# A recommender tower's cross layers: layer 1's fourth unit of products made in halves through PSUM and split in two parts, and the accumulators' banks used by the chunk's parity

## What is computed

```python
for W, b in params:                       # 4096, 8192, 8192 products; 128 outputs each
    z = jnp.einsum('bhd,bfd->bhfd', x_vec, input)
    B, h, f, d = z.shape
    z = z.reshape(B, h * f, d)
    x_vec = jnp.einsum('oc,bcd->bod', W, z) + b[None, :, None]
    outs.append(x_vec.sum(axis=2))
```

## Time and profile before

| | us |
|---|---|
| three runs | 1167.61, 1166.23, 1167.39; median 1167.39 |
| the profiled execution, its own time | 1163.56 |
| its span | 1161.6 |
| busy in the span: TensorE, DVE, POOL, ACT | 1098.8, 1011.0, 905.4, 688.7 |
| TensorE's granted clock over the span | 0.997 |

### The profile page before, as it was taken

One profiled execution on the slowest core, in us unless ns is written; L12 is line 12 of the kernel. 1 busy time (PEld: TensorE's weight loads), 2 busy tenths in 40 slices (PEclk: granted clock), 3 DMA queues, 4 the chain that ended last, 5 costly groups with the idle time before them and its releaser, 6 DMA issues.

```text
span 1161.6 us, 13994 instructions
## 1 busy us (share of the span) xinstructions
PE 1098.8 (95%) x4276; PEld 744.5 (64%) x4276; DVE 1011.0 (87%) x670; ACT 688.7 (59%) x712; POOL 905.4 (78%) x403
## 2 busy tenths in 40 slices
PE   0479999999999999999999999999999999999998
PEld 0246666666666666667666666666676666666696
DVE  4599899999999999989999999999899999998452
ACT  5365466665656656665566666566656566566443
POOL 6469989888988888888988888888889887567000
PEclk9989999999999999999999999999999999999999
DMA  6642415334262525143352524252442525142891
GB/s 239 185 124 66 114 49 153 93 100 145 67 169 75 152 64 161 47 150 94 81 156 73 164 79 136 72 159 57 126 118 79 155 75 159 57 148 88 292 355 41
DMA packets 101789, 142.87 MB, mean 123 GB/s; under 512 B 11746, under 2 KB 55010, under 8 KB 98947
## 3 DMA queue, kind: packets, MB, share of 16 engines
q1 hardware_dynamic: 93570, 140.42, 39.3%
q0 software_dynamic: 8192, 2.11, 2.3%
HBM read 114.96 MB, written 27.53 MB: 123 GB/s over the span
## 4 chain that ended last, share of the span: by engine, by line
PE 84%; POOL 7%; DVE 3%; issue 3%; ACT 2%; DMA 1%; SPq 0%; ACTq 0%; DVEq 0%
PE acc L1110 49%; PE acc L1104 25%; POOL emb L574 3%; POOL z_lo L583 3%; PE z_ps L1251 3%; PE turn_gram_ps L1179 3%; PE z_ps L1241 1%; DVE z L654 1%; DVE z_float L654 1%; ACT x L901 1%; PE turn_gram_ps L1166 1%; DVE z_ps L660 1%; PE acc L1136 1%; DVE z_lo L666 1%; DMA land<-x_scratch 0%
## 5 line engine op out<-in xcount | busy, mean ns | idle before, releaser
L583 POOL TENSOR_TENSOR z_lo<-z,z_hi 128x2048 fp32r<-128x2048 f32 x143 | 659.8, 4615 | 104.4 <-ACT z_hi L864 102.2
L1104 PE MATMUL acc<-z_float,w_sb 128*128 128x512 f32 x768 | 348.7, 600 | 56.8 <-DVE z_float L654 43.2
L1110 PE MATMUL acc<-z_hi,w_hi 128*128 128x512 f32 x896 | 378.3, 422 | 2.5 <-POOL z_lo L583 1.6
L1110 PE MATMUL acc<-z_hi,w_lo 128*128 128x512 f32 x896 | 353.7, 395 | 0.0
L1110 PE MATMUL acc<-z_lo,w_hi 128*128 128x512 f32 x896 | 353.3, 394 | 0.0
L864 ACT ACTIVATE z_hi<-z 128x2048 fp32r<-128x2048 f32 x144 | 275.2, 1911 | 60.5 <-DVE z L654 60.5
L574 POOL DMA_INDIRECT emb<-in_tables,rows_chunk x256 | 245.3, 958 | 63.8 <-issue 56.4
L1104 PEld LDWEIGHTS acc<-z_float,w_sb 128*128 128x128 f32 x768 | 145.7, 192 | 213.0 <-issue 199.0
L873 ACT ACTIVATE z_hi<-z_ps 128x1024 fp32r<-128x1024 f32 x160 | 164.5, 1028 | 127.1 <-PE acc L1110 72.7
L666 DVE TENSOR_TENSOR z_lo<-z_ps,z_hi 128x1024 fp32r<-128x1024 f32 x160 | 194.5, 1216 | 32.5 <-ACT z_hi L873 32.5
L654 DVE TENSOR_TENSOR z<-operand_even,x_shift 128x2048 f32<-128x2048 f32 x80 | 182.9, 2286 | 38.6 <-PE acc L1110 16.2
(11 more groups left out here) (117 smaller groups left out, 631.9 us busy)
## 6 DMA issues: line engine op xcount, KB each, us to landing
land<-x_scratch SPq DMA_DIRECT2D x128, 256.0 KB
land<-x_scratch SPq DMA_DIRECT2D x128, 128.0 KB
x_shift<-x_scratch SPq DMA_DIRECT2D x16, 1024.0 KB, 5.8
gram_scratch<-gram SPq DMA_DIRECT2D x32, 512.0 KB, 6.5
x_shift<-x_scratch SPq DMA_DIRECT2D x16, 768.0 KB, 8.1
z_float<-gram_scratch SPq DMA_DIRECT2D x7, 1024.0 KB, 9.5
x_scratch<-emb SPq DMA_DIRECT2D x32, 192.0 KB, 2.8
x_shift<-gram_scratch SPq DMA_DIRECT2D x6, 1024.0 KB, 6.4
```

What stands on the lines that cost most here:

```text
L583: pool.tensor_tensor(z_lo[:, slot], z[:, slot], z_hi[:, slot].bitcast(F32), ALU.subtract).then_inc(subtracted, 1)
L1104: mm = pe.matmul(acc[:, :], weights[:, tile0 + q, :], z_float[:, g.float_slot(pos), q, :], start=start and q == 0, stop=stop and q == QUAD ...
L1110: mm = pe.matmul(acc[:, :], w[:, tile, :], zz[:, slot, q, :], start=False, stop=stop and n == 2)
```

## The change

Layer 1's position 3 becomes a second unit made in halves. DVE forms it in two halves into `z_ps`, ACT rounds each half, DVE subtracts, and TensorE takes it by `halves_unit` from the same single slot. The subtractions and other products are put in a new order in `layer1_middle`, which now takes up to four pieces of work to place between. Semaphore counts follow (`products`, `halves`, `halves_units`). `z_float` holds one unit a group. The weights of the fourth unit move from the plain to the split arrays, which take 4096 bytes a partition against 2048 before; the area for descriptors of dynamic DMAs shrinks from 8192 to 4096. The two accumulators become `acc[0]` and `acc[1]`: both layers of a chunk use the bank of its parity. Layer 1 of a chunk then waits for x2 of two chunks before, and layer 2 for x1 of the same chunk. In the start, the wait for all split weights moves ahead of layer 1 of chunk 1.

```diff
...
 SPLIT_UNITS = 3
-L1_SPLIT = 2 * QUAD
+L1_SPLIT = SPLIT_UNITS * QUAD
 L2_SPLIT = L2_GROUPS * SPLIT_UNITS * QUAD
 SPLIT_TILES = L1_SPLIT + L2_SPLIT
-L1_PLAIN, L2_PLAIN = 2 * QUAD, L2_GROUPS * QUAD
+L1_PLAIN, L2_PLAIN = QUAD, L2_GROUPS * QUAD
 FLOAT_SLOTS, UNIT_SLOTS = 2, 3
...
+    def products(self, more=0):
+
+        groups, layer1 = self.before()
+        return self.chunk.count(3 * GROUPS - 1, 3 * groups - layer1 + more)
+
+    def halves(self, more=0):
+
+        groups, layer1 = self.before()
+        return self.chunk.count(2 * GROUPS + 2, 2 * groups + 2 * layer1 + more)
+
+    def halves_units(self, more=0):
+
+        groups, layer1 = self.before()
+        return self.chunk.count(GROUPS + 1, groups + layer1 + more)
+
     def unit_slot(self, pos):
...
-    def float_slot(self, pos):
+    def float_slot(self):
         groups, layer1 = self.before()
-        return (groups + layer1 + pos // 3) % FLOAT_SLOTS
+        return (GROUPS * self.chunk.par + groups) % FLOAT_SLOTS
...
-        acc1 = ps("acc1", [P, COLS])
-        acc2 = ps("acc2", [P, COLS])
+        acc = [ps("acc_even", [P, COLS]), ps("acc_odd", [P, COLS])]
...
-                is_float = pos == 0 or pos == 3 and g.is_layer1
-                freed = g.float_freed(pos) if is_float else g.unit_freed(pos)
+                freed = g.unit_freed(pos) if pos else g.float_freed()
                 if freed is not None:
                     dve.wait_ge(used, freed)
-                out = z_float[:, g.float_slot(pos)] if is_float else z[:, g.unit_slot(pos)]
+                out = z[:, g.unit_slot(pos)] if pos else z_float[:, g.float_slot()]
                 dve.tensor_tensor(out, *times(bank, QUAD, x0_tiles), ALU.mult).then_inc(formed, 1)
-            def form_half(g, half, bank, x0_tiles):
-
-                if not g.is_first or half:
-                    dve.wait_ge(halves_split, g.count(2, half))
+            def form_half(g, half, bank, x0_tiles, pos=2):
+
+                n = 2 * (pos - 2) + half
+                if not g.is_first or n:
+                    dve.wait_ge(halves_split, g.halves(n))
                 dve.tensor_tensor(z_ps[:, :, :], *times(bank, 2, x0_tiles), ALU.mult).then_inc(halves_formed, 1)
-            def split_half(g, half):
-
-                dve.wait_ge(halves_rounded, g.count(2, half + 1))
+            def split_half(g, half, pos=2):
+
+                dve.wait_ge(halves_rounded, g.halves(2 * (pos - 2) + half + 1))
                 tiles = slice(2 * half, 2 * half + 2)
...
                 else:
-                    form_half(g, half, pair % 2, x0_shift[:, c.par, 1 + 2 * half:3 + 2 * half])
+                    form_half(g, half, pair % 2, x0_shift[:, c.par, 1 + 2 * half:3 + 2 * half], pos)
...
-            def layer1_middle(c):
-                layer1(c, 2, half=0)
-                layer1(c, 3)
-                split_half(layer1_group(c), 0)
-                layer1(c, 2, half=1)
+            def layer1_middle(c, *between):
+
+                g = layer1_group(c)
+                for n, (pos, half) in enumerate(((2, 0), (2, 1), (3, 0), (3, 1))):
+                    layer1(c, pos, half=half)
+                    if n < len(between):
+                        between[n]()
+                    split_half(g, half, pos)
...
                 split_half(layer2_group(c, 1), 1)
-                sum2(prev)
                 layer1(nxt, 0)
-                split_square(nxt)
-                layer1_middle(nxt)
-                layer2(c, 2, 1)
-                split_half(layer1_group(nxt), 1)
-                layer2(c, 2, 0)
+                layer1_middle(nxt, lambda: split_square(nxt), lambda: sum2(prev),
+                              lambda: layer2(c, 2, 1), lambda: layer2(c, 2, 0))
                 layer2_middle(c, 2)
...
             layer1(c0, 0)
-            split_square(c0)
-
             dve.wait_ge(rounded, 1)
...
                               ALU.subtract).then_inc(subtracted, 1)
-            layer1_middle(c0)
-            split_half(g0, 1)
+            layer1_middle(c0, lambda: split_square(c0))
             layer1(c1, 1)
             layer1(c1, 0)
-            split_square(c1)
-            layer1_middle(c1)
-            split_half(layer1_group(c1), 1)
-            sum1(c0)
+            layer1_middle(c1, lambda: split_square(c1), lambda: sum1(c0))
             layer2(c0, 0, 1)
...
             def released_by_layer2(g, bank):
-                return (formed, g.count(3, 2)) if bank == 0 else (halves_formed, g.count(2, 2))
+                return (formed, g.products(2)) if bank == 0 else (halves_formed, g.halves(2))
             def released_by_layer1(g, bank):
-                return (halves_formed, g.count(2, 2)) if bank == 0 else (formed, g.count(3, 3))
+                return halves_formed, g.halves(2 + 2 * bank)
...
-                act.wait_ge(formed, g.count(3, pos))
+                act.wait_ge(formed, g.products(pos))
                 act.activation(z_hi[:, g.unit_slot(pos)], z[:, g.unit_slot(pos)], ACT.Copy).then_inc(rounded, 1)
-            def round_half(g, half):
-                act.wait_ge(halves_formed, g.count(2, half + 1))
-                if not g.is_first:
+            def round_half(g, half, pos=2):
+                act.wait_ge(halves_formed, g.halves(2 * (pos - 2) + half + 1))
+                if not (g.is_first and pos == 2):
                     if half == 0:
-                        act.wait_ge(half_used, g.count(1))
+                        act.wait_ge(half_used, g.halves_units(pos - 2))
+                    elif pos == 3:
+                        act.wait_ge(used, g.count(4, 3))
                     else:
-                        act.wait_ge(used, g.count(4, -1))
+                        act.wait_ge(used, g.count(4, 0 if g.layer1_at(1) else -1))
                 act.activation(z_hi[:, HALVES_SLOT, 2 * half:2 * half + 2], z_ps[:, :, :], ACT.Copy).then_inc(halves_rounded, 1)
...
                 to_bank(m, 1, 1, released_by_layer2(b, 1))
-                to_bank(m, 2, 0, (formed, m.count(3, 1)))
+                to_bank(m, 2, 0, (formed, m.products(1)))
                 round_unit(m, 1)
-                to_bank(m, 3, 1, (formed, m.count(3, 2)))
+                to_bank(m, 3, 1, (formed, m.products(2)))
                 round_half(m, 0)
...
                 round_half(m, 1)
+                round_half(m, 0, 3)
                 to_bank(d, 1, 1, released_by_layer1(m, 1))
+                round_half(m, 1, 3)
                 round_unit(d, 1)
...
             act.wait_ge(top_in, 6 * 16)
-            for m, bank in enumerate((acc1[:, :], operand[0][:, :], operand[1][:, :], z_ps[:, 0, :])):
+            for m, bank in enumerate((acc[0][:, :], operand[0][:, :], operand[1][:, :], z_ps[:, 0, :])):
                 act.wait_ge(top1_done, m + 1)
...
             act.wait_ge(top3_done, 1)
-            act.activation(y_sb, acc2[0:1, :], ACT.Copy).then_inc(y_ready, 1)
+            act.activation(y_sb, acc[1][0:1, :], ACT.Copy).then_inc(y_ready, 1)
...
         def _(pe):
-            def float_unit(g, acc, weights, tile0, pos=0, start=False, stop=False):
-
-                pe.wait_ge(formed, g.count(3, 2 if pos == 0 else 3))
+            def float_unit(g, acc, weights, tile0, start=False):
+
+                pe.wait_ge(formed, g.products(2))
                 for q in range(QUAD):
-                    mm = pe.matmul(acc[:, :], weights[:, tile0 + q, :], z_float[:, g.float_slot(pos), q, :],
-                                   start=start and q == 0, stop=stop and q == QUAD - 1)
+                    mm = pe.matmul(acc[:, :], weights[:, tile0 + q, :], z_float[:, g.float_slot(), q, :],
+                                   start=start and q == 0, stop=False)
                 mm.then_inc(used, 1)
...
-            def halves_unit(g, acc, tile0):
+            def halves_unit(g, acc, tile0, pos=2, stop=False):
                 for half, done in enumerate((half_used, used)):
-                    pe.wait_ge(halves_split, g.count(2, half + 1))
+                    pe.wait_ge(halves_split, g.halves(2 * (pos - 2) + half + 1))
                     for q in (2 * half, 2 * half + 1):
-                        mm = split_tile(acc, tile0 + q, HALVES_SLOT, q, False)
+                        mm = split_tile(acc, tile0 + q, HALVES_SLOT, q, stop and q == QUAD - 1)
                     mm.then_inc(done, 1)
...
                 g = layer1_group(c)
-                if not c.is_(0):
-                    pe.wait_ge(x1_ready, c.count(1))
-                float_unit(g, acc1, w0_sb, 0, start=True)
-                split_unit(g, 1, acc1, 0)
+                if not (c.is_(0) or c.is_(1)):
+                    pe.wait_ge(x2_ready, c.count(1, -1))
+                float_unit(g, acc[c.par], w0_sb, 0, start=True)
+                split_unit(g, 1, acc[c.par], 0)
                 pe.wait_ge(square_split, c.count(1, 1))
                 for part in range(2):
-                    pe.matmul(acc1[:, :], w_sq[:, part, :], z_sq[:, :], start=False, stop=False)
```

(31 more changed lines are left out.)

30 lines of the change are left out of this document (15 added, 15 removed).

## The result

| | before | after |
|---|---|---|
| median | 1166.32 (6 runs, 1165.95 to 1167.61) | 1271.65 (6 runs, 1267.37 to 1273.98) |
| the profiled execution, own time and span | 1163.56, 1161.6 | 1273.98, 1272.0 |
| granted clock over the span | 0.997 | 0.965 |

The account below looks back on a forecast made before the run. TensorE was taken to bound the kernel, at 64.3 us a round. Twelve intervals at +4.4 (52.8), the last +3.0, start 7.8 and end 3.2 made +66.8 on 1163.56: 1230.4, so a median of 1234; range 1213 to 1264.

Parts of the forecast that it names:

- what the halves and POOL's cycle cost: Chunk 2's m2 to chunk 15's: twelve intervals at +4.4 us (52.8), the last, by TensorE's chain, at +3.0.
- the start: Before the steady rounds: POOL's first layer 2 unit comes later because its product stands behind chunk 1's m3; +7.8 us.
- behind chunk 15's squares: After chunk 15's m2: 8.52 us to d0 where it was 1.40 + 3.47, less an x2 wait; +3.2 us.
- What it adds to DVE and ACT: Each round: DVE gains 2.6 us, to 62.4, plus some 1.8 of waits; ACT gets two roundings of 1.03 us.
- The new wait: At m3's two halves, behind m2 in the single slot: TensorE waits 1.14 and 3.18 us, making a round 67.3.
- What queues behind the wait: ACT's in-order work delays d1: POOL begins it at 7.2 us and closes the cycle at 68.7 us a round.
- Halved descriptor area: POOL's lookups: the smaller area was taken to cost 0, with up to 24 us left to the range.
- The rival that the halves hide: At m3's two gaps: both halves ready in time, only savings stay, about 1148 us; 5%.
- the one that POOL does not close: In the rounds: POOL's pace holds slack the chip does not need; +50 us, a median of 1217; 17%.
- DVE being late elsewhere is excluded by that margin of 3 us: In the rounds: DVE's 62.4 + 1.8 us of its own fits in 67.3, so it reaches the waiting subtraction in time.
- the list of ACT's work behind m3's roundings: ACT's queue in a round: m3's roundings, operand copy, then `round_unit` of d1 (1.91 us), done at about 7.2 us.
- The clock rival: TensorE's clock falls in the new gaps of m3: 2.7 us lost a round, +88, a median of 1255; 26%.

Follow-up runs that it names:

- fill: The changed kernel with DVE's subtraction for the squares' low part replaced by a memset to zeros: 1246.56 us, ratio 1.0709 to the kernel before.
- earlier copy: The changed kernel with the fill, and ACT's second Gram copy moved right behind the first, ahead of d3's rounding: 1242.79 us, ratio 1.0667.
- fillers: 3 and 11 zero-weight matmuls put ahead of TensorE's waits for m3's halves: on the fill alone 1261.14 us, on fill plus earlier copy 1238.12 us.

## Why the prediction was right in kind and wrong in size

The 43.6 us between +66.8 as summed and +110.4 as profiled are found as follows; the terms of the 13 rounds are differences of their landmarks between runs.

| term | forecast | measured |
|---|---|---|
| 13 rounds, what the halves and POOL's cycle cost (fill, earlier copy, fillers) | 55.8 | 59.3 |
| the clock, once the Gram wait is away (earlier copy without and with fillers) | 0 | 2.9 |
| the Gram copy (fill against earlier copy) | 0 | 7.3 |
| z_sq against POOL (change against fill) | 0 | 18.9 |
| the start | 7.8 | 15.6 |
| behind chunk 15's squares | 3.2 | 6.5 |

No run holds the clock still between these rows, so each difference carries some of it: of the 18.9, 2.3 us lie in the two first rounds, whose subtraction is short, and 2.1 of the 7.3 are the two rounds of 70.5. By the subtraction in its old place the z_sq term is 21.3.

**What holds.** "What it adds to DVE and ACT": 2.6 us a round more on DVE, 62.4, measured 62.2 to 62.4. "The new wait": 0.97 and 2.92 for 1.14 and 3.18 in the rounds without a long subtraction. "What queues behind the wait": POOL begins d1 at 758.58, 7.20 after zero, as forecast to the hundredth, and closes the cycle at 68.86 us for 68.7 as soon as nothing else is in the way. "Halved descriptor area": zero. The rival that the halves hide has fallen, and so has the one that POOL does not close.

**The step that failed** is the sentence "DVE being late elsewhere is excluded by that margin of 3 us". It took z_sq at its 0.6 us of the kernel before. The new order puts it behind a product, beside the start of POOL's subtraction, and there it takes 5 us more, which a margin of 3 does not hold. DVE then runs from z_sq to m3 with one gap of 1.0 us and is the bound; the round becomes 72.1 in the mean. This is over half of the miss of 43.6: 18.9 us in the rounds, 3.4 in the start and 0.9 at the end, 23 in all. The profile of before did hold the sign: z_sq's subtractions all took 0.69 us but the last, 3.83, under a running POOL subtraction. The prediction has no sentence on that row.

**The second step that failed** is the list of ACT's work behind m3's roundings, which ended at `round_unit` of d1 because POOL waits for it. The queue goes on: the Gram copy for TensorE stands behind d3's rounding. It was priced at nothing, and the earlier copy gives back 7.3 us in the 13 rounds. A short round is therefore 69.46, made neither by POOL (68.7) nor by TensorE's own chain (67.3), but by the copy: 67.3 + 2.1.

**The start.** With the fill it measured +6.5 in one run (forecast 7.8) but +11.7 to 12.2 in the two later ones with the earlier copy of the Gram matrix. In these and in the change ACT waits some 8 us for an operand's landing and copies it at 51.1 to 51.6 us, where it copied it at 43.83 in the run with +6.5 and at 45.03 in the kernel before. In the eleven experiments that landing goes with the chip: the four runs of one chip have the copy at 43.8 to 45.1, the seven of the other two at 49.9 to 51.7. It does not go with the descriptor area, which three of the four early ones have halved. With the area halved alone it was copied at 51.71, and the first landmark came at 166.08, 3.2 later than in the kernel before, so the changed kernel pays more for it (5.2 and 5.7 us, both runs against the one with +6.5). The profiled executions of before and change are one early and one late, so the late landing itself can't be laid to the edit; its higher price can. z_sq's 4.30 comes on top, worth 3.4 (178.47 against 175.10 with fill and earlier copy). The forecast had no term for either. Without both the start costs 6.5, a little under the 7.8 that was summed.

**The end.** Of the 3.3 us over the forecast 2.5 are the clock's: with the earlier copy the part behind chunk 15's squares took 168.31 us, with the fillers as well, at a granted clock of 1.00 throughout, 165.78, which is 2.75 over the kernel before where 3.2 were forecast.

**The clock rival** (26%) named the fall correctly but not its price of 2.7 us a round. It falls (0.61 in the 4 us from the wait of 2.92 on, in the run with the earlier copy), TensorE loses some 1.6 us, and in the short rounds of the changed kernel that loss comes off a wait that would be there anyway. With the Gram wait away, 13 rounds give 2.9 us back in all when the fall is removed, since then POOL bounds, and the end gives 2.5. The Trainium skill, "TensorE: Matmul & The Clock Gate", section "Why this matters for your kernels", warns of idle gaps that bring back the lower rate; the trace now shows the fall behind waits of 1.9 and 2.9 us, in most rounds and not in all, and that it need not cost time.

## What to carry to other kernels

When an edit changes the order on one engine, look up for each moved instruction what other engines run at its new time, not only for its duration at the old one: an outlier in the trace of before (3.83 against 0.69 us) is a price list. Follow an in-order queue behind a new wait to its end, for every consumer and not only for the nearest one. And judge a stall by what waits behind it: the lower clock was free ahead of a wait for ACT and cost 1.55 us a round once it fell behind that wait.

## What was not expected of the hardware

- In the changed kernel VectorE's 64x512 subtraction with both inputs in SBUF took 5.3 to 5.75 us in place of 0.69 where POOL's subtraction of 4.6 us began, by the records, up to 0.65 us after it. At 596.63 it ended at 602.16, which is 0.56 us behind POOL's. So the one whose record starts first did not win: its record seems to hold a wait for the port. The Trainium skill, "SBUF — State Buffer", section "🔬 SBUF: two separate sides", says that whichever starts first gets the shared pair; by the start times of the records that does not come out here. One thing goes with it: in all 14 such cases of the change, of the run with d0 later and of that with three half slots, POOL's subtraction follows its lookup at once (0.02 us). In the kernel before, in that with parity alone and in that with the descriptor area alone, POOL's subtraction at the start had waited over 17 us for ACT; it starts 0.40 us behind DVE's, and there DVE's takes 0.68 or 0.69 (63.78 and 64.18 above). So a POOL instruction that stands ready in its queue may hold the pair before its record starts; no run tests that.
- With the fillers, a wait of 1.90 us that ended at 261.80 was followed by a granted clock of 0.57; the same wait one round later, ended at 332.83, with TensorE as busy in the 4 us before its end (2.10 us both times), was followed by 1.00. The length of the wait does not decide it alone.
